# Three PSUM banks for the maximum tiles, batch steps in the value product's bank, and inverse roots of seven batches by a power on GpSimd

## The chip, the cores and the metric

The kernel runs on one core of one Trainium2 chip. The time is device microseconds of that core, the median of the runs.

## The reference

A pre-norm transformer layer on x of shape 8 x 512 x 128 in float32. `xn` is the layer norm of x. For each of 16 heads there are keys and queries of width 128 and values of width 8; scores q k / sqrt(128) under a causal mask, softmax, times v, the heads joined and multiplied by Wp, plus bp, plus x. The result is normed again: each row is centred and multiplied by 1/sqrt(variance + 1e-5). Then follows a mixture of experts: a shared feed-forward part, and 8 routed experts of which each row takes the 2 with the highest sigmoid of its logit, weighted by the normalised scores. Both are added to the row.

```
x = x + attention(layernorm(x))
x = x + shared(layernorm(x)) + sum over top-2 experts of w * down(silu(gate) * up)
```

## The kernel before, in words

The five engines run one program each, all laid out over the same numbered **slots** (`for t in range(SLOTS)`). There are 128 heads in all (8 batches x 16 heads, `UNITS`). In slot t:

- TensorE projects head t (L982 to L984, three float16 products: high times high, high times low, low times high) into bank 0. Then it scores head t - 10 for the softmax in three tiles (L1040 to L1042, banks 3 to 5), and between these tiles head t - 1 for its row maxima in three tiles k = 0, 1, 2 (L1019), with 512, 384 + 128 and 256 columns. Tile number n = 3u + k goes to bank 1 or 2, by n % 2, and waits until tile n - 2 has been reduced.
- ScalarE copies the projection to `qh` (L1264) and makes the exponentials of head t - 10 (L1299).
- VectorE writes the low half `ql` from the bank and `qh` (L1399), and reduces the maximum tiles (L1427, with an accumulator read that belongs to each). The next projection waits for `ql`.
- GpSimd zeroes what is above the diagonal of the exponentials (L914, L916).

Every fourth slot (t = 3 modulo 4, from slot 15: `PV_AT`) TensorE first multiplies four heads' exponentials with the values (`weigh_values`, L1056) into bank 6, and ScalarE copies the bank to `oT` (L1289) and stores it. In these slots VectorE reduces the maxima last, after all other work of the slot; in the others it reduces them ahead of that work. One slot earlier (t = 2 modulo 4, from slot 6) TensorE transposes the row maxima of four heads (L1215, "low"), VectorE casts them to `lowT` (L1407), and SyncE takes them through HBM into row 0 of `qh`.

The work that follows a batch is spread over the slots after its last head by hand-written offsets (`STEPS` for batches 0 to 6, `LAST_STEPS` for batch 7, `PART_STEPS` for the sorting of rows by expert), counted from slot 29 + 16b: "rinv" on VectorE (L1486), "mult" on GpSimd (L937), "proj" on TensorE (L1074) and VectorE (L1366), "stats" and "aggr" on VectorE (L1495, L1499), then the inverse root of the variance on VectorE: a seed from the bits (L108 to L111), three Newton steps (L116 to L119) in slots +6 and +7, a scaling (L1506). "norm" (+8) writes `hn` on GpSimd (L944), "split" (+10) its high half on ScalarE (L1252) and its low half on VectorE (L1391), and "logits" (+14) the router's product. "count", "rank" and "place" give each row its place among its expert's rows (L1104, L1114 to L1118, L1553 to L1572). All small products of this kind, "low", "proj", "logits", "count", "rank", the shared weights' transposes (L1007, slots 8 and 9) and the sum of the weights' squares, use bank 7 in turn: `turn` makes each wait until the last was taken (`t_taken`), and who reads it waits for `t_filled`.

```
T_USES = sorted([(LOW_AT + GROUP * g, "low", g) for g in range(GROUPS)] + [(W_SUM_AT, "w_sum", 0)]
X_BANK, V_BANK, SCALE_LINKS = (3, 4), (5, 6), 6
```

In slots 1 to 8 the batches are transposed (L992) and their values made (L1001, banks 5 and 6 by turns). GpSimd adds the bias to x in slots 11 to 18 (L908), and VectorE makes low halves of the projection's weights (L1432) until slot 13. From slot 138 (`FFN_AT`) on the feed-forward part runs, in banks 0 to 7, beside the last batch's steps.

## Time and profile before

| | |
|---|---|
| median of 3 runs | 730.77 us (729.43 to 732.49) |
| span of the profiled execution | 730.7 us, and no other time is given for that execution |
| TensorE busy (matmuls) | 654.0 us |
| VectorE busy | 541.8 us |
| ScalarE busy | 456.8 us |
| GpSimd busy | 310.2 us |
| first and last projection (L982) | 27.8 and 501.4 us |

In the profile PE is TensorE's matmuls, PEld its weight loads, DVE VectorE, ACT ScalarE, POOL GpSimd and SP SyncE. Lines are those of the kernel before. Matmuls overlap, so what one adds to the time is the distance between two starts, not its own duration.

### The profile page before, as it was taken

Reading aid. Unit: us, or ns where it says so; the run is one execution under the profiler, and the core shown is the slowest. Engines: PE = TensorE matmul, PEld = TensorE weight load, DVE = VectorE, ACT = ScalarE, POOL = GpSimd, SP = SyncE. Lnnn points to the kernel's source line nnn. Section 1 sums busy time; section 2 is a strip of 40 time slices with the busy share of each in tenths; the row PEclk is TensorE's granted clock in tenths of the full one; section 3 lists DMA queues with packets and bytes.
Section 4 is the critical chain, followed back from the end, with each engine's and each line's share of the span. In section 5 each row is a group of like instructions: output and inputs, shape, how many; then the busy total and the mean of one; then the engine's idle time right before and its main releaser. Section 6 shows DMA issues by size and latency. Waiting matters only on the chain.

```text
span 730.7 us, 16418 instructions
## 1 busy us (share of the span) xinstructions
PE 654.0 (90%) x5432; PEld 398.4 (55%) x5432; DVE 541.8 (74%) x1903; ACT 456.8 (63%) x816; POOL 310.2 (42%) x512
## 2 busy tenths in 40 slices
PE   7488999999999999998899999999986779899992
PEld 6264455545554554554445455455565568777652
DVE  6699877787788778788877877868546655567796
ACT  3376676767667776765676776666762545565651
POOL 4493531314123223221477522313465356565773
PEclk9699999999999999999999999999998889999997
DMA  9100443621122101221132111021444257695424
GB/s 255 53 2 20 133 128 105 175 77 45 49 74 44 32 32 42 77 70 37 49 93 85 45 51 42 17 44 64 102 107 107 73 117 145 126 164 120 110 60 126
DMA packets 102768, 60.24 MB, mean 82 GB/s; under 512 B 44568, under 2 KB 94640, under 8 KB 102688
## 3 DMA queue, kind: packets, MB, share of 16 engines
q1 hardware_dynamic: 66144, 28.22, 16.2%
q10 hardware_dynamic: 32336, 22.29, 10.4%
q0 software_dynamic: 4208, 8.69, 4.6%
q8 instruction: 47, 0.77, 0.4%
q14 instruction: 33, 0.27, 0.1%
HBM read 19.62 MB, written 30.77 MB: 69 GB/s over the span
## 4 chain that ended last, share of the span: by engine, by line
PE 63%; DVE 17%; ACT 6%; issue 6%; another core or an unknown queue 2%; POOL 1%; ACTq 0%; DVEq 0%; POOLq 0%
PE bank L1019 8%; PE bank L1040 7%; PE bank L1056 7%; PE bank L1042 6%; PE bank L1041 6%; DVE junk L1427 5%; PE bank L1136 4%; PE bank L1138 4%; PE bank L1137 4%; PE bank L982 3%; PE bank L984 3%; PE bank L983 3%; DVE ql L1399 3%; ACT p_sb L1299 2%
## 5 line engine op out<-in xcount | busy, mean ns | idle before, releaser
L1299 ACT ACTIVATE p_sb<-bank,inv_scale 128x512 f32<-128x512 f32 (+1 forms) x384 | 222.0, 614 | 40.6 <-PE bank L1042 33.3
L1427 DVE CUSTOM_DVE_ANT_0 junk<-bank,causal 128x512 bf16<-128x512 f32 (+3 forms) x512 | 221.8, 483 | 31.4 <-PE bank L1019 29.0
L914 POOL TENSOR_SCALAR_AFFINE_SELECT p_sb<-p_sb 128x384 f32<-128x384 f32 x128 | 67.0, 524 | 306.5 <-ACT p_sb L1299 305.9
L1041 PE MATMUL bank<-ql,ah 128*128 128x512 f16 (+3 forms) x512 | 153.4, 300 | 0.0
L1042 PE MATMUL bank<-qh,al 128*128 128x512 f16 (+3 forms) x512 | 153.0, 300 | 0.0
L1019 PE MATMUL bank<-ah,qh 128*128 128x512 f16 (+3 forms) x512 | 132.5, 303 | 21.8 <-DVE low L1427 20.3
L1040 PE MATMUL bank<-qh,ah 128*128 128x512 f16 (+3 forms) x512 | 147.2, 300 | 0.8 <-ACT p_sb L1299 0.8
L1399 DVE TENSOR_TENSOR ql<-bank,qh 128x512 f16<-128x512 f32 x128 | 88.5, 691 | 64.7 <-ACT qh L1264 61.3
L1264 ACT ACTIVATE qh<-bank 128x512 f16<-128x512 f32 x128 | 76.5, 597 | 62.4 <-PE bank L984 60.3
L1611 DVE SCALAR_TENSOR_TENSOR al<-bank,gu_scale,ah 128x512 f32<-128x512 f32 x69 | 51.6, 748 | 61.3 <-ACT ah L1330 41.9
L1019 PEld LDWEIGHTS bank<-ah,qh 128*128 128x128 f16 x512 | 50.1, 98 | 79.7 <-DVE low L1427 47.6
L1330 ACT ACTIVATE ah<-bank,inv_gate 128x512 f32<-128x512 f32 x69 | 47.4, 686 | 68.9 <-PE bank L1138 40.9
L962 POOL DMA_INDIRECT p_sb<-ys_dram,place x64 | 69.9, 1092 | 37.2 <-PE bank L1138 14.2
L953 POOL DMA_INDIRECT xs_dram<-rows,place x64 | 65.6, 1025 | 42.4 <-issue 14.4
L1056 PE MATMUL bank<-p_sb,v_sb 128*9 128x512 f32 (+3 forms) x1024 | 74.9, 433 | 0.3 <-POOL p_sb L916 0.3
L1040 PEld LDWEIGHTS bank<-qh,ah 128*128 128x128 f16 x512 | 50.2, 98 | 40.8 <-issue 8.3
L1042 PEld LDWEIGHTS bank<-qh,al 128*128 128x128 f16 x512 | 50.1, 98 | 25.0 <-issue 0.3
L1136 PE MATMUL bank<-mh,wh 128*128 128x256 f16 x212 | 60.3, 284 | 3.3 <-issue 1.6
L1138 PE MATMUL bank<-mh,wl 128*128 128x256 f16 x212 | 60.2, 284 | 2.1 <-issue 2.0
L1041 PEld LDWEIGHTS bank<-ql,ah 128*128 128x128 f16 x512 | 50.2, 98 | 21.7 <-issue 0.3
L1137 PE MATMUL bank<-ml,wh 128*128 128x256 f16 x212 | 60.0, 283 | 1.7 <-issue 1.7
L1174 PE MATMUL bank<-wh,qh 128*128 (+1 forms) x276 | 53.6, 227 | 6.3 <-ACT ql L1325 2.7
(247 smaller groups left out, 1130.2 us busy)
## 6 DMA issues: line engine op xcount, KB each, us to landing
o_dram<-oT ACTq DMA_DIRECT2D x32, 256.0 KB, 2.3
ys_dram<-ql ACTq DMA_DIRECT2D x25, 256.0 KB
xs_dram<-causal ACTq DMA_DIRECT2D x6, 832.0 KB, 4.8
wst<-in_Wkqv SPq DMA_DIRECT2D x8, 264.0 KB, 5.0
x_sb<-in_x SPq DMA_DIRECT2D x8, 256.0 KB, 5.8
out<-x_sb SPq DMA_DIRECT2D x8, 256.0 KB
o_all<-o_dram SPq DMA_DIRECT2D x7, 256.0 KB
r_all<-r_dram SPq DMA_DIRECT2D x7, 256.0 KB
```

The lines of the kernel that those rows point to most:

```text
L1019: last = nc.tensor.matmul(m.psum[M_BANK[n % 2]][:, at:at + w], qh[:, u % RING, i * P:(i + 1) * P], m.ah[:, seg(b, N, w)], start=True, stop ...
L1040: nc.tensor.matmul(bank, m.ah[:, keys], qh[:, s, c * P:N], start=True, stop=False)
L1041: nc.tensor.matmul(bank, m.ah[:, keys], ql[:, s, c * P:N], start=False, stop=False)
L1042: last = nc.tensor.matmul(bank, m.al[:, keys], qh[:, s, c * P:N], start=False, stop=True)
L1056: last = nc.tensor.matmul(m.psum[O_BANK][32 * j:32 * j + V1, c * P:N], m.v_sb[:, v // H * TB + c, v % H, :], p_sb[v % P_RING][:, P_AT[c]:P ...
L1136: nc.tensor.matmul(out, hi, x_h, start=True, stop=False)
L1137: nc.tensor.matmul(out, hi, x_l, start=False, stop=False)
L1138: return nc.tensor.matmul(out, lo, x_h, start=False, stop=True)
L1264: nc.scalar.activation(qh[:, t % RING, :], m.psum[Q_BANK][:, :], ACT.Copy).then_inc(qh_ready, 1)
L1299: nc.scalar.activation(p_sb[v % P_RING][:, S_AT[k]:S_AT[k] + S_WIDTH[k]], m.psum[S_BANK[k]][:, 0:S_WIDTH[k]], ACT.Exp, scale=m.inv_scale[: ...
L1399: nc.vector.tensor_tensor(ql[:, t % RING, :], m.psum[Q_BANK][:, :], qh[:, t % RING, :], ALU.subtract).then_inc(ql_ready, 1)
L1427: last = nc.vector.tensor_tensor_reduce(out=junk[:, (3 * u + k) % 2, at:at + w], in0=m.psum[M_BANK[(3 * u + k) % 2]][:, at:at + w], in1=m. ...
```

## The change

The maximum tiles get one bank each, 1, 2 and 7, and tile k waits for tile k of the head before. Until slot 138 the small products that used bank 7 use bank 6, the value product's; from then on bank 7. So `turn` now also waits, until slot 138, for the last copy of the value product (in slots up to 9 for the values' copy or the bank's clearing), after it for the last maximum; and `weigh_values`, and the values' products that use bank 6, wait until the small products before them are taken. The steps that met the value product's slots move: logits +14 to +15, rank and place +26 to +27, send +27 to +28, the shared weights' transposes from slots 8 and 9 to 11 and 12. `same_head` now shares its memory with `ones`, and is made by GpSimd in slot 50 instead of slot 10, by two instructions instead of three. `junk` is [128, 1280], a part for each tile. For batches 0 to 6 the inverse root leaves VectorE; GpSimd computes (variance + eps) ** -0.5 ahead of "norm" in two instructions on 128 x 4. Batch 7 keeps the old way.

```diff
+        self.same_head = self.ones
...
-STEPS = {"rinv": 0, "mult": 2, "proj": 4, "stats": 6, "aggr": 6, "newton0": 6, "newton1": 7, "newton2": 7, "norm": 8, "split": 10, "logits": 14}
+STEPS = {"rinv": 0, "mult": 2, "proj": 4, "stats": 6, "aggr": 6, "newton0": 6, "newton1": 7, "newton2": 7, "norm": 8, "split": 10, "logits": 15}
...
-PART_STEPS = {"sort": 18, "weigh": 22, "count": 23, "rank": 26, "place": 26, "expert": 30, "send": 27}
+PART_STEPS = {"sort": 18, "weigh": 22, "count": 23, "rank": 27, "place": 27, "expert": 30, "send": 28}
...
+SAME_HEAD_AT = W_SUM_AT + 2
...
-SHARED_T_AT = B
+SHARED_T_AT = LAG + 1
...
-    Q_BANK, M_BANK, S_BANK, O_BANK, T_BANK = 0, (1, 2), (3, 4, 5), 6, 7
+    Q_BANK, M_BANK, S_BANK, O_BANK, T_BANK = 0, (1, 2, 7), (3, 4, 5), 6, 7
...
+    def t_bank(t):
+
+        return m.psum[O_BANK if t < FFN_AT else T_BANK]
...
+            nc.gpsimd.memset(minus_half[:, :], -0.5).then_inc(low_clear, 1)
+            pool.wait_ge(low_clear, 3)
...
                 if (b := batch_at("norm", t)) is not None and b < B - 1:
+                    pool.wait_ge(spread_known, b + 1)
+                    nc.gpsimd.tensor_scalar(raised[:, :], m.stats[:, seg(b, TB), 1], EPS, None, ALU.add).then_inc(var_raised, 1)
+                    pool.wait_ge(var_raised, b + 1)
+                    nc.gpsimd.tensor_tensor(m.rstd[:, seg(b, TB)], raised[:, :], minus_half[:, :], ALU.pow).then_inc(rstd_ready, 1)
                     pool.wait_ge(rstd_ready, b + 1)
...
+                if V_BANK[b % 2] == O_BANK and turns_before(b + 2) > 0:
+                    pe.wait_ge(t_taken, turns_before(b + 2))
...
-                if n >= 2:
-                    pe.wait_ge(max_ready, n - 1)
+                if u >= 1:
+                    pe.wait_ge(max_ready, n - 2)
...
             def weigh_values(g):
                 pe.wait_ge(p_masked, 2 * GROUP * (g + 1))
 
+                pe.wait_ge(t_taken, turns_before(min(PV_AT + GROUP * g, FFN_AT)))
...
             def turn(name, n):
+                at = T_USES[T_TURN[name, n]][0]
                 if T_TURN[name, n] > 0:
                     pe.wait_ge(t_taken, T_TURN[name, n])
+                if at >= FFN_AT:
+                    pe.wait_ge(max_ready, 3 * UNITS)
+                elif at > PV_AT:
+                    pe.wait_ge(oT_ready, weighed_before(at))
+                elif at > B + 1:
+                    pe.wait_ge(o_clear, 1)
+                else:
+                    pe.wait_ge(v_ready, at - at % 2 - 2)
...
-                    post.link(last)
-                    rsqrt_seed(nc, post.link, m.stats[:, seg(b, TB), 1], var[:, :], m.rstd[:, seg(b, TB)], tmp[:, :])
+                    if b < B - 1:
+                        last.then_inc(spread_known, 1)
+                    else:
+                        post.link(last)
+                        rsqrt_seed(nc, post.link, m.stats[:, seg(b, TB), 1], var[:, :], m.rstd[:, seg(b, TB)], tmp[:, :])
                 for step in range(RSQRT_STEPS):
-                    if (b := batch_at(f"newton{step}", t)) is not None:
+                    if (b := batch_at(f"newton{step}", t)) == B - 1:
```

## Rows read from the trace of the kernel before

**Rows 1.** the busy shares of the whole span (engine, us, share, instructions).

```profile
PE 654.0 (90%) x5432; PEld 398.4 (55%) x5432; DVE 541.8 (74%) x1903; ACT 456.8 (63%) x816; POOL 310.2 (42%) x512
```

**Rows 2.** busy us by stretch, 79.2 to 501.4; then PE clock, DMA share, GB/s.

```profile
79.20:501.40 422.20, 408.09 (x3179) 215.25 (x3180) 330.65 (x1281) 291.06 (x515) 141.39 (x282) 1.00 0.23 66
```

**Rows 3.** the waits from 79.2 to 501.4: us, times, longest.

```profile
DVE ql L1399 <- ACT qh L1264: 55.8, 95, 1.4
...
PEld bank L1019 <- DVE low L1427: 36.6, 85, 2.8
...
PE bank L1019 <- DVE low L1427: 13.1, 19, 2.5
```

**Rows 4.** timeline of slot 40 and its neighbours: start, length, [idle before].

```profile
172.50 0.38 PE L982 MATMUL bank<-ah,mh 128*128 128x512 f16 x1
...
175.10 0.27 PE L1042 MATMUL bank<-qh,al 128*128 128x256 f16 x1
...
175.19 0.08 DVE L1427 DVE_READ_ACCUMULATOR2_ANT low<- 128x1 f32 x1
...
175.32 0.10 PEld L1019 LDWEIGHTS bank<-ah,qh 128*128 128x128 f16 x1 [0.23 <-DVE low L1427]
...
175.33 0.28 PE L1019 MATMUL bank<-ah,qh 128*128 128x256 f16 x1
...
175.45 0.38 PE L982 MATMUL bank<-ah,mh 128*128 128x512 f16 x1
...
176.22 0.08 DVE L1427 DVE_READ_ACCUMULATOR2_ANT low<- 128x1 f32 x1
...
176.92 0.69 DVE L1399 TENSOR_TENSOR ql<-bank,qh 128x512 f16<-128x512 f32 x1 [0.62 <-ACT qh L1264]
...
178.28 0.28 PE L1019 MATMUL bank<-ah,qh 128*128 128x256 f16 x1
```

**Rows 5.** timeline of slot 35, the first with a batch's statistics.

```profile
155.68 0.17 DVE L108 TENSOR_SCALAR var<-stats 128x4 f32<-128x4 f32 x1
...
156.96 0.69 DVE L1427 CUSTOM_DVE_ANT_0 junk<-bank,causal 128x512 bf16<-128x512 f32 x1
...
157.72 0.28 PE L1019 MATMUL bank<-ah,qh 128*128 128x256 f16 x1 [0.90 <-DVE low L1427]
```

**Rows 6.** TensorE at the end of slot 83, and the stretch behind it.

```profile
339.82 0.39 PE L1019 MATMUL bank<-ah,qh 128*128 128x256 f16 x1 [2.51 <-DVE low L1427]
...
340.00:344.00 4.00, 4.00 (x18) 1.85 (x17) 2.38 (x10) 1.35 (x3) 0.00 (x0) 0.62 0.00 0
```

**Rows 7.** VectorE's chain of rank and place, first and last instruction.

```profile
527.32 0.20 DVE L1553 TENSOR_TENSOR above<-ranks,full_tiles 128x48 f32<-128x48 f32 x1
...
529.86 0.18 DVE L1572 CAST place<-slot 128x24 int32<-128x24 f32 x1
```

**Rows 8.** timeline of hn, its split and oT, batches 0 and 6.

```profile
165.03 3.16 POOL L944 TENSOR_SCALAR hn<-x_sb,stats,rstd 128x128 f32<-128x128 f32 x4
...
168.64 0.62 ACT L1252 ACTIVATE rows<-hn 128x512 f16<-128x512 f32 x1
...
170.45 0.60 ACT L1289 ACTIVATE oT<-bank 128x512 f32<-128x512 f32 x1 [1.19 <-PE bank L1056]
...
526.05 0.63 ACT L1252 ACTIVATE rows<-hn 128x512 f16<-128x512 f32 x1 [2.31 <-POOL hn L944]
```

**Rows 9.** timeline of slot 6, the values' product and the cast.

```profile
50.59 1.06 PE L1001 MATMUL bank<-wv,wh 128*128 128x128 f32 x8
...
51.48 0.27 DVE L1407 CAST lowT<-bank 16x128 f16<-16x128 f32 x1
```

**Rows 10.** the waits of the whole span.

```profile
DVE ql L1399 <- ACT qh L1264: 61.3, 106, 1.5
```

**Rows 11.** groups of GpSimd by shape: busy us, mean ns.

```profile
L310 POOL COPY wv<-wst 128x16 f32<-128x16 f32 x8 | 1.8, 223 | 5.6 <-DMA wst<-in_Wkqv 5.6
...
L908 POOL TENSOR_TENSOR x_sb<-x_sb,bp_bc 128x512 f32<-128x512 f32 x8 | 10.2, 1273 | 0.0
```

More of the change, by code:

```diff
@@ L533, with turns_before, weighed_before @@
 T_TURN = {(name, n): i for i, (_, name, n) in enumerate(T_USES)}
+def turns_before(t):
+    return sum(1 for at, _, _ in T_USES if at < t)
+def weighed_before(t):
+    return sum(1 for g in range(GROUPS) if PV_AT + GROUP * g < t)
+assert not any(group_at(at, PV_AT) is not None for at, _, _ in T_USES if at < FFN_AT)
 X_RING, GU_RING, LATE, DEEP = 4, 6, 4, 3
@@ L725, in body @@
     var = sb("var2", [P, TB], F32)
+    raised = sb("raised", [P, TB], F32)
+    minus_half = sb("minus_half", [P, TB], F32)
     tmp = sb("tmp2", [P, TB], F32)
@@ L1013, in score_for_max @@
                     pe.wait_ge(qh_ready, u + 1)
-                if n >= 2:
-                    pe.wait_ge(max_ready, n - 1)
+                if u >= 1:
+                    pe.wait_ge(max_ready, n - 2)
                 for i, at in MAX_TILES[k]:
                     w = (i + 1) * P
-                    last = nc.tensor.matmul(m.psum[M_BANK[n % 2]][:, at:at + w], qh[:, u % RING, i * P:(i + 1) * P], m.ah[:, seg(b, N, w)], start=True, stop=True)
+                    last = nc.tensor.matmul(m.psum[M_BANK[k]][:, at:at + w], qh[:, u % RING, i * P:(i + 1) * P], m.ah[:, seg(b, N, w)], start=True, stop=True)
                 last.then_inc(max_scored, 1)
@@ L1067, in after_attention @@
                     pe.wait_ge(w_sq_ready, 1)
-                    nc.tensor.matmul(bank_t[:, 0:KINDS], m.ones[:, :], w_sq[:, :], start=True, stop=True).then_inc(t_filled, 1)
+                    nc.tensor.matmul(t_bank(t)[:, 0:KINDS], m.ones[:, :], w_sq[:, :], start=True, stop=True).then_inc(t_filled, 1)
                 if (b := batch_at("proj", t)) is not None:
@@ L1073, in after_attention @@
                     for i in range(TB):
-                        last = nc.tensor.matmul(bank_t[:, i * P:(i + 1) * P], onT[:, i * P:(i + 1) * P], m.wp[:, :], start=True, stop=True)
+                        last = nc.tensor.matmul(t_bank(t)[:, i * P:(i + 1) * P], onT[:, i * P:(i + 1) * P], m.wp[:, :], start=True, stop=True)
                     last.then_inc(t_filled, 1)
@@ L1078, in after_attention @@
                     pe.wait_ge(late_r_ready, 1)
-                    pe.wait_ge(same_head_made, 3)
-                    nc.tensor.matmul(bank_t[:, :], m.same_head[:, :], r_all[:, :], start=True, stop=True).then_inc(t_filled, 1)
+                    pe.wait_ge(same_head_made, 2)
+                    nc.tensor.matmul(t_bank(t)[:, :], m.same_head[:, :], r_all[:, :], start=True, stop=True).then_inc(t_filled, 1)
                 if late_at("late", t):
@@ L1084, in after_attention @@
                     for i in range(TB):
-                        last = nc.tensor.transpose(bank_t[:, i * P:(i + 1) * P], hn[:, i, :], m.ident[:, :])
+                        last = nc.tensor.transpose(t_bank(t)[:, i * P:(i + 1) * P], hn[:, i, :], m.ident[:, :])
                     last.then_inc(t_filled, 1)
@@ L1103, in after_attention @@
                     for c, (t0, t1) in enumerate(CHUNKS[g]):
-                        last = nc.tensor.matmul(bank_t[0:(t1 - t0) * E, c * P:(c + 1) * P], picked[:, t0:t1, :].rearrange("p t e -> p (t e)"), m.ones16[:, :], start=True, stop=True)
+                        last = nc.tensor.matmul(t_bank(t)[0:(t1 - t0) * E, c * P:(c + 1) * P], picked[:, t0:t1, :].rearrange("p t e -> p (t e)"), m.ones16[:, :], start=True, stop=True)
                     last.then_inc(t_filled, 1)
@@ L1110, in after_attention @@
                     for c, (t0, t1) in enumerate(CHUNKS[g]):
-                        rank = bank_t[:, c * P:c * P + rows[c]]
+                        rank = t_bank(t)[:, c * P:c * P + rows[c]]
                         for d in range(c):
@@ L1117, in after_attention @@
                     for c in range(len(rows)):
-                        last = nc.tensor.matmul(bank_t[:, at:at + E], totals[0:rows[c], base + c, :], m.earlier[0:rows[c], CHUNK, :], start=(c == 0), stop=(c == len(rows) - 1))
+                        last = nc.tensor.matmul(t_bank(t)[:, at:at + E], totals[0:rows[c], base + c, :], m.earlier[0:rows[c], CHUNK, :], start=(c == 0), stop=(c == len(rows) - 1))
                     last.then_inc(t_filled, 1)
@@ L1214, in _ @@
                     turn("low", g)
-                    nc.tensor.transpose(bank_t[:, 0:P], low[g % 2][:, :], m.ident[:, :]).then_inc(t_filled, 1)
+                    nc.tensor.transpose(t_bank(t)[:, 0:P], low[g % 2][:, :], m.ident[:, :]).then_inc(t_filled, 1)
                 if 1 <= t < B:
```

44 lines of the change are left out of this document (20 added, 24 removed).

## The prediction

> **What bounds the kernel now.** Read the busy shares first: TensorE is busy 90% of the span, VectorE 74%, ScalarE 63%, GpSimd 42% [rows 1]. Then the stretches: from 79.2 to 501.4 us, heads 15 to 126, TensorE is busy 408.1 of 422.2 us at a granted clock of 1.00 (2.4 GHz) [rows 2]. So TensorE sets the pace there, and what can be won is its stalls. The waits of that stretch name one: the matmuls of L1019 (scores for the row maxima) wait for VectorE's reductions of L1427, 36.6 us in 85 waits seen at the weight load and 13.1 us in 19 seen at the matmul [rows 3].
>
> These two are not to be added, since one stall shows at both. And the 85 waits start too early: a weight load is issued ahead. In an ordinary slot the last score matmul starts at 175.10 and would have let L1019 start at 175.21 (each 256-column matmul follows the last by 0.11); VectorE reads its accumulator from 175.19 to 175.27, L1019 starts at 175.33, and the next slot at 175.45 [rows 4]. The loss is 0.12 us of a slot of 2.95 (172.50 to 175.45), where the weight load's wait says 0.23. With 0.11 taken off each, 36.6 - 85 x 0.11 = 27.3 us is the real loss in this stretch.
>
> **The three maximum banks.** Two banks serve three tiles per head, so tile 2 waits for tile 0 of its own head. In rows 4 that tile is read just when it is wanted. With a bank per tile it waits for tile 2 of the head before, which VectorE has left at 176.30 (176.22 + 0.08) where the next slot's L1019 starts at 178.28. The margin goes from -0.12 to about 1.8 us.
> - Ordinary slots: about 84 outside the value product's own, 84 x 0.12 = 10.1 us. I take all. Next in line is ql: VectorE is done with a slot at 176.30 and starts ql at 176.92 [rows 4], when qh comes; 0.62 us less the 0.12 that the slot shrinks leaves 0.5, so VectorE still keeps up.
> - Slots with batch work on VectorE hold the other 27.3 - 10.1 = 17.2 us. In slot 35 the maxima start at 156.96 and L1019 waits 0.90 [rows 5]. The third bank alone covers this. The worst is slot 83, with a wait of 2.51 us, after which the clock is granted at 0.62 (part of the time at 1.2 GHz) for 4 us [rows 6]; those 4 us hold some 1.5 us more, if matmuls run 0.62 as fast, in a slot that the 27.3 us don't count.
>
> What stays: rank and place move to the plain slot 88, behind the maxima. Their chain takes 2.7 us (527.32 to 530.04) [rows 7]; the free time behind the maxima is 0.5, and ql may end some 0.8 us later before the next projection waits. 2.7 - 1.3 = 1.4 us stays, about what it costs now. For other heavy slots where VectorE's own work is too long I leave 2.1 us. Gain of the stretch: 27.3 - 1.4 - 2.1 = **23.8 us**, and I leave the 1.5 us of the clock as a reserve.
>
> Bounds of this term: 10.1 (only the even stall goes) and 28.8 (all, with the clock).
>
> **The shared bank.** The low transpose sits one slot ahead of the value product, and the other steps move to other slots, so each pair lies a slot apart. VectorE takes such a tile some 1.5 us before the product wants the bank; ScalarE copies oT right when the product ends, two slots ahead of the next low transpose. The logits, count and rank steps come one slot behind the product, whose copy starts at 170.45 [rows 8], in the same slot. Price 0; if a take is late, each of 28 groups loses up to the 0.27 us of a cast [rows 9], 7.6 us.
>
> **The first 15 slots.** There VectorE is nearly full, and its wait for qh is 61.3 - 55.8 = 5.5 us outside the stretch [rows 3, 10], since a late L1019 delays the next projection. I take half, 2.7 us won. Against it: in slot 6 the values' matmuls start at 50.59 but must now wait until lowT is cast at 51.75 [rows 9], 1.2 us; and the shared weights' transposes move into slots 11 and 12, for which I take 0.5 us between nothing and another 1.2 of the same kind. Net **+1.0**, between -1.2 and +3.
>
> **The inverse root.** From VectorE seven times: seed, Newton steps and scaling, thirteen instructions; the part in slot 35 is 155.68 to 156.96, 1.28 us [rows 5]. That sits in the stalls counted above, so it gets no credit of its own: either part alone removes them, and they overlap. To GpSimd come an add and a power, each 128x4. No row shows a power. Nearest in size is the copy of 128x16, 0.22 us; nearest as a two-input operation is L908 over 512 elements, 1.27 us [rows 11]. Two instructions: 0.45 to 2.5 us. I take 1.0, since four elements are nearer the copy, but a power is more than a copy. Nothing excludes that it is far dearer, which is a rival below.
>
> What hides it: GpSimd writes hn from 165.03 to 168.19, ScalarE takes it at 168.64 and then idles 1.19 us before oT [rows 8]. Slack 0.45 + 1.19 = 1.64, less 0.12 for a shorter slot: 1.5 us. Under it, batches 0 to 5 cost nothing. Behind the waits on GpSimd are the next head's masks, which the product wants several slots later. Batch 6 has no slack: ScalarE waits 2.31 us for hn at 526.05 [rows 8] on the chain that ended last. There the 1.0 us is paid: **-1.0**.
>
> The Trainium skill (GPSIMD Engine Reference, Specifications and Performance versus the Vector engine) says that GpSimd is about half as fast at elementwise work and shares its SBUF interfaces with VectorE where an instruction has two SBUF inputs. By it the move is the wrong way; at four elements it would still be covered by the slack.
>
> **The sum.** 23.8 + 1.0 - 1.0 = 23.8 us off the profiled execution's 730.7, **706.9 us**. The median of the runs is 730.77, so nothing shifts. Work after 501.4 is unchanged and simply starts earlier.
>
> **The rivals.**
> 1. *The power is dear.* Place: GpSimd ahead of hn; hn late, so ScalarE's split, oT and the exponentials late. Price for an add and power of X: 6 x (X - 1.5) + (X - 1.0) more than my sum. At X = 3, 718; at 6, 739. It cancels the gain at 7X = 33.8, X = 4.8 us, and from 5.4 the kernel is slower by over 0.5%. For: no row prices a power, and a GpSimd pass can cost 1.27. Against: it is four elements. Chance 0.13 for X over 2.5, of which 0.07 beyond 5.4 and 0.02 within 0.5% of no change.
> 2. *A new wait eats half.* The shared bank loses 0.27 us per group (7.6), and 3 to 4 us of heavy slots stay because ql, not the maxima, is what is late there: 718. For: VectorE's margin is but 0.5. Against: the places lie a slot apart. Chance 0.13.
> 3. *TensorE is not what is short.* The stalls turn up elsewhere, at qh or the exponentials, because the same VectorE and ScalarE latencies close the loop: 728, within 0.5%. Against: TensorE is busy 408.1 of 422.2 us, and VectorE 330.7 of them [rows 2]. Chance 0.04.
>
> 4. *The first power alone is slow.* If it takes as long as the four instructions of hn, 3.16 us [rows 8], slot 37 is late by 3.16 - 1.5 = 1.7 us once: 708.6. Against: nothing in the trace shows a first instruction of its kind to be longer. Chance 0.05. The Trainium skill (GPSIMD Engine Reference, Instruction dispatch) has the first call of newly loaded code pay about 6 us; by it slot 37 would lose some 4.5 us, an estimate from that page, for 711.4.
>
> The forecast holds 0.65. Half a per cent, 3.7 us, is what can be told from no change. Faster: 0.65 + 0.13 + 0.05 + 0.04 of rival 1 = 0.87; same 0.04 + 0.02 = 0.06; slower 0.07. The range runs from 701 (all stalls, with the clock) to 722 (rival 2, and the power up to 3.5 us).
>
> **What would show it.** Right: L1019's waits for L1427 nearly gone from the stretch, ordinary slots 2.82 to 2.83 us, no idle time before L1019 in slot 83 and no clock below 1.00 behind it, the stretch from head 15's projection to the last near 398 us. Power: the duration of its row, and whether ScalarE waits for hn more than once. Shared bank: no waits of L1056 or L1215 on oT or lowT. Wrong: ordinary slots still 2.95, or as much idle time in front of L982.

## The result, and the profile after

The kernel after takes 708.49 us (707.27 to 710.94 in 4 runs) where the kernel before takes 730.96 (729.43 to 732.49 in 4 runs): a ratio of 0.9683, 95% interval 0.9647 to 0.9719. The forecast was 706.9 us, and the range 701 to 722 holds the result. The profiled execution has a span of 709.0 us and a time of its own of 710.94, so it is 2.5 us above the median; spans below are compared with spans (730.7 before).

Where the 21.7 us between the spans come from, counted at the first matmul of each head's projection (the interval from one head's projection to the next is called a slot here; a value slot is one with the value product, a low slot the one ahead of it, with the transpose of the maxima, and any other is an ordinary slot):

| Stretch | Before | After | Difference |
|---|---|---|---|
| start to head 0's projection | 27.8 | 28.8 | +1.0 |
| slots 0 to 14 | 51.5 | 49.4 | -2.1 |
| slots 15 to 126 | 422.2 | 395.4 | -26.8 |
| last projection to the end | 229.3 | 235.5 | +6.2 |

So the stretch with heads gained 3 us more than forecast, and the part behind it lost some 5 us more. The busy shares of the kernel after, which answer to [rows 1], from its profile page:

```profile
PE 642.9 (91%) x5432; PEld 406.0 (57%) x5432; DVE 525.1 (74%) x1812; ACT 454.1 (64%) x816; POOL 318.1 (45%) x526
```

VectorE has 91 instructions fewer, GpSimd 14 more. The stretches by busy time (us, then busy us and count of TensorE, its weight loads, VectorE, ScalarE, GpSimd, then clock, DMA share, GB/s), the first of which answers to [rows 2]:

```profile
78.13:473.48 395.35, 393.66 (x3181) 220.65 (x3179) 317.91 (x1205) 287.94 (x516) 150.16 (x296) 1.00 0.24 71
473.48:709.00 235.52, 190.76 (x1888) 142.32 (x1885) 145.13 (x351) 123.05 (x214) 126.35 (x137) 0.94 0.46 108
```

TensorE now idles 1.7 us of the 395.4; before it was 14.1 of 422.2. What it waited for there, from the waits of this stretch at the matmuls (us, times, longest), against the 13.1 us in 19 of [rows 3]:

```profile
PE bank L1006 <- DVE ql L1435: 1.3, 1, 1.3
...
PE bank L1045 <- DVE low L1463: 0.2, 1, 0.2
```

L1045 is the old L1019, L1463 the old L1427, L1006 the old L982. The 36.6 us in 85 waits at L1019's weight load are gone from this stretch. The one wait that is left, 1.3 us, is in slot 89, where VectorE's chain of rank and place stands ahead of ql. The same ordinary slot 40 as in [rows 4], from the timeline:

```profile
166.84 0.38 PE L1006 MATMUL bank<-ah,mh 128*128 128x512 f16 x1
...
169.44 0.27 PE L1068 MATMUL bank<-qh,al 128*128 128x256 f16 x1
...
169.55 0.27 PE L1045 MATMUL bank<-ah,qh 128*128 128x256 f16 x1
169.55 0.10 PEld L1006 LDWEIGHTS bank<-ah,mh 128*128 128x128 f16 x1
169.66 0.38 PE L1006 MATMUL bank<-ah,mh 128*128 128x512 f16 x1
```

L1045's last tile now follows the last score matmul by 0.11 us (169.44, 169.55) and the slot is 2.82 us long where it was 2.95. Slot 83 has gone from 7.95 to 5.20, the length of a plain slot with a value product.

The inverse root, from the groups by shape (busy us, mean ns):

```profile
L962 POOL TENSOR_TENSOR rstd<-raised,minus_half 128x4 f32<-128x4 f32 x7 | 7.3, 1045 | 0.6
L960 POOL TENSOR_SCALAR raised<-stats 128x4 f32<-128x4 f32 x7 | 1.7, 238 | 0.0
```

and for batch 0 from the timeline of GpSimd (this view ends after two of hn's four instructions):

```profile
160.12 0.24 POOL L960 TENSOR_SCALAR raised<-stats 128x4 f32<-128x4 f32 x1
160.45 1.05 POOL L962 TENSOR_TENSOR rstd<-raised,minus_half 128x4 f32<-128x4 f32 x1
161.61 1.61 POOL L968 TENSOR_SCALAR hn<-x_sb,stats,rstd 128x128 f32<-128x128 f32 x2
```

A power on 128x4 costs 1.05 us, and with the add and the two handovers hn starts 1.49 us later (160.12 to 161.61) than it would without them. The first power is as long as the others.

### The profile page after: what moved, and what is told of

It is laid out like the page before. It is cut to its first block, busy times and chain, and to the rows that moved or that the text cites. A ratio compares the mean times of both kernels' runs of the same rounds, so it can differ in the third digit from the quotient of the medians.

```text
span 709.0 us, 16346 instructions
## 1 busy us (share of the span) xinstructions
PE 642.9 (91%) x5432; PEld 406.0 (57%) x5432; DVE 525.1 (74%) x1812; ACT 454.1 (64%) x816; POOL 318.1 (45%) x526
## 4 chain that ended last, share of the span: by engine, by line
PE 69%; DVE 9%; POOL 7%; issue 5%; ACT 4%; another core or an unknown queue 2%; ACTq 0%; DVEq 0%; POOLq 0%
PE bank L1066 8%; PE bank L1083 8%; PE bank L1045 8%; PE bank L1068 8%; PE bank L1067 8%; PE bank L1174 4%; PE bank L1172 4%; PE bank L1006 3%; PE bank L1007 3%; PE bank L1008 3%; PE bank L1173 3%; POOL xs_dram L977 3%; DVE junk L1463 2%; PE bank L1210 2%; PE bank L1211 2%
## 5 line engine op out<-in xcount | busy, mean ns | idle before, releaser
L1463 DVE CUSTOM_DVE_ANT_0 junk<-bank,causal 128x512 bf16<-128x512 f32 (+3 forms) x512 | 221.8, 483 | 27.1 <-PE bank L1045 26.3
L1045 PE MATMUL bank<-ah,qh 128*128 128x512 f16 (+3 forms) x512 | 130.1, 301 | 0.4 <-DVE low L1463 0.4
L986 POOL DMA_INDIRECT p_sb<-ys_dram,place x64 | 68.3, 1066 | 38.4 <-PE bank L1174 15.3
L1083 PE MATMUL bank<-p_sb,v_sb 128*9 128x512 f32 (+3 forms) x1024 | 74.9, 433 | 0.3 <-POOL p_sb L937 0.3
L1045 PEld LDWEIGHTS bank<-ah,qh 128*128 128x128 f16 x512 | 50.2, 98 | 34.3 <-issue 1.6
L1210 PE MATMUL bank<-wh,qh 128*128 (+1 forms) x276 | 53.3, 226 | 13.5 <-ACT ql L1361 7.5
```

Of the source, the lines that this page charges most:

```text
L1045: last = nc.tensor.matmul(m.psum[M_BANK[k]][:, at:at + w], qh[:, u % RING, i * P:(i + 1) * P], m.ah[:, seg(b, N, w)], start=True, stop=True)
L1083: last = nc.tensor.matmul(m.psum[O_BANK][32 * j:32 * j + V1, c * P:N], m.v_sb[:, v // H * TB + c, v % H, :], p_sb[v % P_RING][:, P_AT[c]:P ...
L1463: last = nc.vector.tensor_tensor_reduce(out=junk[:, S_AT[k] + at:S_AT[k] + at + w], in0=m.psum[M_BANK[k]][:, at:at + w], in1=m.causal[:, N ...
```

## The experiments

Twelve runs were made of ten different kernels, in three sets of four, each set on one chip beside the kernel before. Six powers and six powers with the values swapped were measured in two of the sets, and the kernel after once more. Ratios are to the kernel before of the same set, whose median was 732.19 us for the first set and 734.88 for the other two. The chips differ (the kernel before takes 732.19 us on one and 734.88 on the others), so between sets the ratios are to be compared and not the times. "To last" is the time from head 15's projection to the last one, "tail" from the last projection to the end of the span, both of the profiled run.

| Kernel | us | Ratio (95%) | To last | Tail |
|---|---|---|---|---|
| before | 732.19 / 734.88 | 1 | 422.2 | 229.3 |
| after, first measurement | 708.49 | 0.9683 (0.9647-0.9719) | 395.4 | 235.5 |
| banks only | 707.26 | 0.9667 (0.9632-0.9702) | 399.1 | 227.6 |
| power only | 730.05 | 0.9972 (0.9948-0.9996) | 416.2 | 234.3 |
| two banks | 726.49 | 0.9940 (0.9912-0.9969) | 413.3 | 229.1 |
| six powers | 703.97 | 0.9625 (0.9592-0.9658) | 395.2 | 228.1 |
| six powers, values swapped | 706.05 | 0.9603 (0.9574-0.9632) | 396.4 | 229.6 |
| powers thrice | 717.80 | 0.9776 (0.9740-0.9811) | 405.8 | 230.4 |
| last batch by a power too | 707.76 | 0.9617 (0.9573-0.9660) | 395.4 | 231.7 |
| place later | 711.09 | 0.9666 (0.9623-0.9708) | 395.0 | 237.7 |
| batch 6's power alone | 714.50 | 0.9732 (0.9705-0.9759) | 399.0 | 236.4 |
| after, again | 709.59 | 0.9651 (0.9631-0.9671) | 396.1 | 235.1 |
| six powers, again | 706.28 | 0.9611 (0.9591-0.9631) | 396.1 | 230.1 |
| values swapped, again | 704.30 | 0.9583 (0.9564-0.9602) | 397.4 | 231.6 |

### One part at a time: the banks only

```diff
                 if (b := batch_at("norm", t)) is not None and b < B - 1:
-                    pool.wait_ge(spread_known, b + 1)
-                    nc.gpsimd.tensor_scalar(raised[:, :], m.stats[:, seg(b, TB), 1], EPS, None, ALU.add).then_inc(var_raised, 1)
-                    pool.wait_ge(var_raised, b + 1)
-                    nc.gpsimd.tensor_tensor(m.rstd[:, seg(b, TB)], raised[:, :], minus_half[:, :], ALU.pow).then_inc(rstd_ready, 1)
...
-                    if (b := batch_at(f"newton{step}", t)) == B - 1:
+                    if (b := batch_at(f"newton{step}", t)) is not None:
```

(the seed and the closing scale come back for all batches in the same way).

> The three banks and the batch steps in the value product's bank, but all eight inverse roots on VectorE as before. Theory (the banks carry the gain, either part alone frees the heavy slots): every slot is as short as with the whole change, 2.82 ordinary and 5.20 value slots, slot 83 included; the chain of Newton steps hides behind TensorE; batch 6's 1.5 us in the tail comes back, so 705.5 to 708.5, most likely 707. Rival (the root's move is what freed the heavy slots): slots 35, 51, 67, 83 and 99 keep 0.7 to 2.7 us each of their stalls, some 12 to 17 us in all, so 718 to 725.

Measured: 707.26 us, 0.9667. The time is the theory's, the slots are so only nearly: slots 35, 51, 67, 83, 87 and 99 are all 5.20, but slots 84 (4.50 instead of 2.88), 85 (3.72 for 2.82) and 53 (3.49 for 2.83) stay long, and the stretch is 399.1 us, 3.8 above the kernel after. The timeline of TensorE in slot 84:

```profile
326.87 0.38 PE L1041 MATMUL bank<-ah,qh 128*128 128x512 f16 x1 [1.02 <-DVE low L1459]
```

and of VectorE ahead of it (a Newton step, and the chain of the weights behind it):

```profile
324.03 0.15 DVE L119 SCALAR_TENSOR_TENSOR rstd<-tmp,rstd 128x4 f32<-128x4 f32 x1
...
325.74 0.25 DVE L1580 TENSOR_TENSOR weight<-top 128x12 f32<-128x12 f32 x2
326.02 0.69 DVE L1459 CUSTOM_DVE_ANT_0 junk<-bank,causal 128x512 bf16<-128x512 f32 x1
```

The third bank gives TensorE one slot of room, not more: VectorE is more than a slot late here, the Newton steps being part of what is queued ahead of the maxima. So taking seven roots off VectorE is worth these 3.8 us when the banks are there, and 2.9 in the one pair below that was measured on one chip.

### The power only

```diff
@@ the kernel before
-                    post.link(last)
-                    rsqrt_seed(nc, post.link, m.stats[:, seg(b, TB), 1], var[:, :], m.rstd[:, seg(b, TB)], tmp[:, :])
+                    if b < B - 1:
+                        last.then_inc(spread_known, 1)
+                    else:
+                        post.link(last)
+                        rsqrt_seed(nc, post.link, m.stats[:, seg(b, TB), 1], var[:, :], m.rstd[:, seg(b, TB)], tmp[:, :])
```

with the add and the power on GpSimd as in the change.

> The kernel before with seven of its inverse roots by a power on Pool and nothing else of the change. Theory (either part alone frees the heavy slots): slots 35, 51, 67, 83, 87 and 99 fall to 5.20 to 5.4 us, the ordinary slots stay at 2.95 with their wait of TensorE for the reduction; 17 us less in the stretch, 1.5 more for batch 6 behind it, so 713 to 718, most likely 715. Rival (the heavy slots stall on the second bank's turn whatever VectorE has in its queue there): they keep most of it and the time is 724 to 731.

Measured: 730.05 us, 0.9972: the rival was right in the time, and the theory wrong. The slots show neither reason alone. 35, 51, 67 and 99 do fall to 5.20 (from 5.93 to 6.56) and 84 and 85 to 3.14 and 2.95. But 83 keeps 6.33, 87 grows from 6.83 to 8.29 and 88 from 2.95 to 4.50, and 39, 71 and 103 each grow by 0.5 to 0.6. In slot 88 TensorE is busy throughout, at a granted clock of 0.62: that growth is the clock behind the wait of slot 87. Slot 84's old length had held the same kind of fall, with 0.65 granted. From TensorE's timeline:

```profile
334.73 0.28 PE L1027 MATMUL bank<-ah,qh 128*128 128x256 f16 x1 [0.95 <-DVE low L1435]
352.25 0.28 PE L1027 MATMUL bank<-ah,qh 128*128 128x256 f16 x1 [2.82 <-DVE low L1435]
```

Slot 83 still has statistics, weight splits and the sort of a whole part ahead of its maxima; slot 87 has rank and place, and now in front of them VectorE's own wait for the split of hn, 1.06 us, since hn comes later:

```profile
347.51 0.69 DVE L1399 SCALAR_TENSOR_TENSOR rows<-hn,rows 128x512 f16<-128x512 f32 x1 [1.06 <-ACT rows L1260]
```

So with two banks the power takes away one queue and lengthens another: it gains 6.0 us in the stretch, and 5.0 of them are lost again in the tail (229.3 to 234.3).

### The third bank taken away

```diff
-    Q_BANK, M_BANK, S_BANK, O_BANK, T_BANK = 0, (1, 2, 7), (3, 4, 5), 6, 7
+    Q_BANK, M_BANK, S_BANK, O_BANK, T_BANK = 0, (1, 2), (3, 4, 5), 6, 7
...
-                if u >= 1:
-                    pe.wait_ge(max_ready, n - 2)
+                if n >= 2:
+                    pe.wait_ge(max_ready, n - 1)
...
-                    last = nc.tensor.matmul(m.psum[M_BANK[k]][:, at:at + w], qh[:, u % RING, i * P:(i + 1) * P], m.ah[:, seg(b, N, w)], start=True, stop=True)
+                    last = nc.tensor.matmul(m.psum[M_BANK[n % 2]][:, at:at + w], qh[:, u % RING, i * P:(i + 1) * P], m.ah[:, seg(b, N, w)], start=True, stop=True)
```

> The whole change but for the third bank: the maximum tiles alternate between two banks as before, the batch steps stay in the value product's bank and the power on Pool. Theory: 10 us of ordinary slots come back (0.12 to 0.13 each in some 84), and what the third bank alone gives in the heavy slots; 717 to 722, most likely 719, with TensorE's wait for VectorE before the maximum products back at some 30 us or more. Rival (the third bank gives the ordinary slots nothing, their shortening comes from elsewhere, such as the batch steps): within 2 us of the kernel after, 707 to 711.

Measured: 726.49 us, 0.9940, above the expected 717 to 722. The direction is the theory's: ordinary slots are back at 2.95, low slots at 3.14. The size is larger, since the third bank is worth 17.9 us in the stretch (413.3 against 395.4) and 3.8 in the first 15 slots (53.2 against 49.4), of which only some 10 are the even stall, the 0.12 us or so that every ordinary slot loses. TensorE's waits for VectorE before the maxima came back as 12.9 us at the matmul and 38.0 at the weight load (over the whole span, where the kernel after has 0.4 and 0.8):

```profile
PEld bank L1045 <- DVE low L1463: 38.0, 90, 1.9
PE bank L1045 <- DVE low L1463: 12.9, 20, 1.6
```

Beside the power-only kernel this one also prices the shared bank and the moved steps: they cost 1.7 us in the first 15 slots (slots 6 and 10 are 1.4 longer each) and gain 2.9 in the stretch, mostly because rank and place left the value slot (87 to 89 together are 13.5 us for 15.7) and the logits steps left theirs (43, 59 and so on are 5.20 for 5.48).

### Batch 6's root back on VectorE

```diff
                 if (b := batch_at("norm", t)) is not None and b < B - 1:
+                    if b < B - 2:
+                        pool.wait_ge(spread_known, b + 1)
...
-                    if (b := batch_at(f"newton{step}", t)) == B - 1:
+                    if (b := batch_at(f"newton{step}", t)) is not None and b >= B - 2:
```

> The kernel after with batch 6's inverse root back on VectorE, six powers left. Theory (that power stands on the path behind the last projection and, as TensorE idles there, costs clock too): the last exponentials come 1.5 to 3 us earlier after the last projection (33.8 in the kernel after, 30.7 before) and the time is 705.5 to 707.5, most likely 706.5. Rival (the offset is set by the later gaps in the feed forward part, not by batch 6): the start of the feed forward part moves, the end does not, and the time is 708 to 709.5.

Measured: 703.97 us, 0.9625, which is 1.5 us below the range given, and beside the kernel after on one chip (third set) 706.28 us against 709.59. The direction is the theory's, and the last exponentials do come 3.1 us earlier. In the kernel after, the chain in the tail reads, for ScalarE and TensorE:

```profile
499.59 0.63 ACT L1288 ACTIVATE rows<-hn 128x512 f16<-128x512 f32 x1 [3.79 <-POOL hn L968]
...
500.85 0.20 PE L1150 MATMUL bank<-earlier,totals 96*128 96x96 f16 x1 [1.76 <-ACT oT L1325]
```

and with batch 6's root on VectorE:

```profile
496.08 0.63 ACT L1289 ACTIVATE rows<-hn 128x512 f16<-128x512 f32 x1 [2.30 <-POOL hn L969]
...
497.34 0.20 PE L1151 MATMUL bank<-earlier,totals 96*128 96x96 f16 x1 [0.27 <-ACT oT L1326]
```

ScalarE waits 1.49 us longer for hn, which is the handover of the power; oT and the exponentials queue behind it, so TensorE stands 1.49 us longer too. Then the clock: the windows from 25 us after the last projection, two of 5 us each, first of the kernel after:

```profile
498.50:503.50 5.00, 2.92 (x21) 1.72 (x20) 2.81 (x10) 3.79 (x7) 2.58 (x6) 0.92 0.46 132
503.50:508.50 5.00, 4.67 (x29) 2.69 (x31) 0.51 (x3) 3.58 (x6) 1.75 (x5) 0.74 0.23 52
```

with six powers:

```profile
496.50:501.50 5.00, 4.41 (x35) 2.67 (x34) 3.31 (x12) 4.95 (x10) 1.81 (x6) 1.00 0.47 132
501.50:506.50 5.00, 4.66 (x54) 2.68 (x53) 0.75 (x1) 2.61 (x4) 3.50 (x5) 1.00 0.32 81
```

and with two banks and the same power for batch 6:

```profile
519.30:524.30 5.00, 2.92 (x23) 1.67 (x21) 2.74 (x10) 3.80 (x7) 2.65 (x6) 1.00 0.47 133
524.30:529.30 5.00, 4.66 (x48) 2.58 (x49) 1.33 (x4) 4.20 (x7) 3.00 (x6) 1.00 0.26 61
```

TensorE is busy 2.92 us of the first window in the first and the third, 4.41 in the second. In the kernel after the granted clock then falls to 0.92 and 0.74, which is 3.4 us in all at 1.2 GHz (0.8 in the first window, 2.6 in the second), and TensorE gets 29 matmuls done in the second window where it does 48 in the two-bank kernel, which idles as long and keeps its clock, and 54 with six powers. ScalarE's first silu of the feed-forward part dates the effect in every profile: 30.7 us after the last projection in the nine profiles of kernels with batch 6's root on VectorE, 32.2 in the two-bank kernel (the handover alone), and 33.8 or 33.9 in the four with the power and a clock below 1.00 (after twice, power only, batch 6's power alone). Their tails are 234.3 to 236.4 us. The two-bank kernel's is 229.1, within those without the power (227.6 to 231.7, place later aside). So of the 3.1 us by which the first silu is late, 1.5 are the handover and 1.6 the clock. (3.4 us at half the clock hold what full speed does in 1.7, so 1.7 is the most that it can cost.) From the silu to the end these four take 200.6 to 202.5 us and the others, place later aside, 196.9 to 201.0. This further difference of some 2 us, which makes up the 5 us of tail seen in the profiles, isn't explained. And that the fall of the clock is worth 1.6 us rests on a single profile of the two-bank kernel.

### The six powers' worth, and batch 6's alone

The edit is shown against the kernel with six powers.

```diff
-                    if b < B - 2:
+                    if b == B - 2:
...
-                    if (b := batch_at(f"newton{step}", t)) is not None and b >= B - 2:
+                    if (b := batch_at(f"newton{step}", t)) is not None and b != B - 2:
```

> Three banks, and a power on POOL for batch 6 alone; the batches 0 to 5 have their roots on VectorE as before. Theory (batch 6's power is all loss, the other six are all gain): the slots are those of the kernel with the banks only (84, 85, 53, 37, 69 and 101 longer by 3.8 us together than in the kernel after), the tail is that of the kernel after (first silu of the feed forward part 33.8 us after the last projection, not 30.7), so it is the slowest of this set, 3 to 4 us above the kernel after on the same chip, near 712. Rival (batch 6's power costs its 1.5 us and the rest of the loss in the tail is chance of the runs): 1.5 us above the kernel with the banks only, near the kernel after, 708 to 709.

> The kernel after, unchanged, on the same chip as the three others of this set. Theory: 4 to 5 us above the kernel with six powers, 3 to 4 below the one with batch 6's power alone. Rival (batch 6's power costs only its handover): 1.5 us above the kernel with six powers.

> The kernel with six powers, batch 6's root on VectorE, beside the kernel after on one chip. Theory: 0.6 per cent (4 to 5 us) faster than it. Rival: 0.2 per cent.

Measured on one chip: 714.50, 709.59 and 706.28 us. The order is the theory's; the sizes are not quite. Batch 6's power costs 3.3 us (709.59 to 706.28, ratios 0.9651 and 0.9611, whose intervals just meet, while the slowest of the five runs with six powers, 706.98, is below the fastest of the other five, 707.85). That lies between the theory's 4 to 5 and the rival's 1.5, and agrees with the 3.1 us seen at the first silu. Between sets the ratios give 4.2 us (0.9683 less 0.9625) and 4.8 (0.9732 less 0.9667) for the same power. The other six powers gain 4.9 us (714.50 to 709.59, intervals apart), of which 2.9 to 3.6 can be read in the stretch (399.0 against 396.1 and 395.4). The two nearly cancel in the kernel after, which is why it does not differ from the banks only: 0.9651 and 0.9683 against 0.9667.

### How much room the power has

The edit is against the kernel with six powers.

```diff
-                        nc.gpsimd.tensor_tensor(m.rstd[:, seg(b, TB)], raised[:, :], minus_half[:, :], ALU.pow).then_inc(rstd_ready, 1)
+                        nc.gpsimd.tensor_tensor(m.rstd[:, seg(b, TB)], raised[:, :], minus_half[:, :], ALU.pow).then_inc(var_raised, 1)
+                        pool.wait_ge(var_raised, 3 * b + 2)
+                        nc.gpsimd.tensor_tensor(m.rstd[:, seg(b, TB)], raised[:, :], minus_half[:, :], ALU.pow).then_inc(var_raised, 1)
+                        pool.wait_ge(var_raised, 3 * b + 3)
+                        nc.gpsimd.tensor_tensor(m.rstd[:, seg(b, TB)], raised[:, :], minus_half[:, :], ALU.pow).then_inc(rstd_ready, 1)
```

> The kernel with six powers, each of them run three times in a row, so 2.09 us more on POOL ahead of each batch's rows. By the prediction's price (six times what the power exceeds its slack of 1.5 us; the handover now takes 1.48) that costs 6 times 2.07, 12.4 us, so 716. Rival (a batch's rows have more room than 1.5 us since three banks leave VectorE and ScalarE ahead of TensorE): under 2 us, 704 to 706, with ScalarE's wait for the rows some 2 us longer each time and no value slot above 5.3.

Measured: 717.80 us, 0.9776. Against 0.9625 and 0.9611 for the same kernel with single powers that is 1.5% of 734.88 us, 11 to 12 us, where the prediction's formula gives 12.4. Slots 40, 56, 72, 88, 104 and 120 are longer by 1.8, 1.3, 1.7, 1.6, 2.2 and 1.3 us, 10.0 in all, each at a granted clock of 1.00. The timeline at slot 40:

```profile
167.20 0.63 ACT L1293 ACTIVATE rows<-hn 128x512 f16<-128x512 f32 x1 [3.90 <-POOL hn L973]
...
169.04 0.38 PE L1071 MATMUL bank<-qh,ah 128*128 128x512 f16 x1 [1.17 <-ACT p_sb L1340]
```

ScalarE stands 3.90 us for hn with oT and the exponentials behind it, and TensorE waits for the exponentials. From the first power's start to hn it is 3.33 us in that slot (160.67 to 164.00) where a single power takes 1.16 (160.45 to 161.61 above), so 2.17 us are added, and 10.0/6 = 1.67 of them is lost: 1.49 + 2.17 - 1.67 = 2.0 us is the room for add and power, on the mean of the six. The prediction had 1.5. The single power uses three quarters of it.

### Slot 6: the values in the other bank

Slot 6 went from 3.39 us to 6.50 in the kernel after. Its rows, which answer to [rows 9]:

```profile
51.43 0.27 DVE L1443 CAST lowT<-bank 16x128 f16<-16x128 f32 x1
...
51.84 1.81 PE L1027 MATMUL bank<-wv,wh 128*128 128x128 f32 x8 [1.48 <-DVE lowT L1443]
...
53.45 1.27 PE L1045 MATMUL bank<-ah,qh 128*128 128x512 f16 x4
```

The wait is 1.48 us, and behind it the same matmuls take longer: 1.81 us for eight of the values' product (1.06 before) and 1.27 for the four of the maxima (0.71 in the kernel with six powers and the swap, below). The granted clock of slot 6 is 0.81:

```profile
48.01:54.51 6.50, 4.21 (x22) 2.89 (x21) 4.36 (x14) 3.12 (x7) 6.42 (x7) 0.81 0.02 5
```

The first profile of six powers has the same wait of 1.48 us and a clock of 1.00 in slots 6 and 7, which take 5.34 and 2.53 us there against 6.50 and 3.02: the fall of the clock costs 1.7 us. It does not always come in slot 6. Of the nine profiles with the shared bank and the values not swapped, five show it there, three in slot 10 (4.5 to 4.6 us there, for 2.94) and one in neither.

The swap, against the kernel with six powers:

```diff
-    X_BANK, V_BANK, SCALE_LINKS = (3, 4), (5, 6), 6
+    X_BANK, V_BANK, SCALE_LINKS = (3, 4), (6, 5), 6
...
-                    pe.wait_ge(v_ready, at - at % 2 - 2)
+                    pe.wait_ge(v_ready, at - at % 2 - 1)
```

> The kernel with six powers, and the values of the batches 0, 2, 4, 6 instead of 1, 3, 5, 7 in the bank that the transposes of the minima share, so that in slot 6 the transpose and batch 5's values lie in different banks. Theory (slot 6 grew from 3.39 to 5.34 and 6.50 us because TensorE waits 1.48 us for VectorE's copy out of the shared bank and its clock falls behind the wait): slot 6 falls to 3.0 to 3.6 us, the time by 1.5 to 2.5 us to 702, unless the wait reappears in slot 7, where batch 6's values follow the transpose into the same bank; there the copy is a slot old. Rival (the first slots are bound by the chain of transposes, ScalarE's copies and POOL's rows, whatever the bank): slots 5 to 8 keep their sum and the time stays within 0.7 us of 704.

> Six powers and the banks of the values swapped, beside the same on one chip. Theory: slots 5 to 8 together are 1.5 to 2 us shorter than in the kernel with six powers, and the time is 1 to 2 us below it, the fastest of this set, since nothing behind the first slots changes. Rival: the feed forward part takes up the gain, no difference.

Measured: 706.05 us, 0.9603, where the kernel without the swap had 0.9625 in the first set, and on the third set 704.30 us, 0.9583, against 706.28, 0.9611. The timeline of slot 6 in the second of them:

```profile
50.27 1.06 PE L1028 MATMUL bank<-wv,wh 128*128 128x128 f32 x8
...
51.16 0.71 PE L1046 MATMUL bank<-ah,qh 128*128 128x512 f16 x4
51.50 0.27 DVE L1444 CAST lowT<-bank 16x128 f16<-16x128 f32 x1
51.70 0.38 PE L1007 MATMUL bank<-ah,mh 128*128 128x512 f16 x1
```

The product no longer waits for the cast, the clock stays, and the slot takes 3.62 us. Slot 7 gets longer (3.69 for 2.53 to 3.02), so slots 5 to 8 together are only 0.6 us shorter than with six powers (13.46 for 14.02), and not the 1.5 to 2 expected. Slots 0 to 14 take 47.1 to 47.2 us with the swap and 48.2 to 49.7 without; most of that is the clock, which falls in slot 6 or 10 in all but one of the profiles without the swap, and in neither slot in the three with it. This has the lowest ratio of the study, 0.9583 (0.9564 to 0.9602), though its interval overlaps with that of six powers. Its lead of 2.0 us over the one without the swap is about what such runs can tell; both pairs of runs point the same way.

### The last batch by a power too

The edit is against the kernel with six powers.

```diff
+                if late_at("norm", t):
+                    pool.wait_ge(spread_known, B - 1)
+                    nc.gpsimd.tensor_scalar(raised[:, :], m.stats[:, seg(B - 1, TB), 1], EPS, None, ALU.add).then_inc(var_raised, 1)
+                    pool.wait_ge(var_raised, B - 1)
+                    nc.gpsimd.tensor_tensor(m.rstd[:, seg(B - 1, TB)], raised[:, :], minus_half[:, :], ALU.pow).then_inc(rstd_ready, 1)
                 for g, i, k in sends_at(t):
```

> The kernel with six powers, and the last batch's root also by a power on POOL (batch 6's alone stays on VectorE). TensorE waits 4.2 us for that batch's normalised rows, behind a chain of 14 small instructions on VectorE. Theory (what counts is the length of the chain against the handover): the chain takes 3.9 us from 527.85 to 531.73 with two feed forward instructions between, add and power 1.5, so the rows come up to 1.5 us earlier and the time falls by up to 1.5 to 702.5 to 704. Rival (POOL issues row sends at that point, 1.0 to 1.4 us each behind TensorE's progress, and the power queues behind one of them): the rows come 0 to 3 us later and the time is 704 to 708.

Measured: 707.76 us, 0.9617, the same as with six powers. TensorE's wait for that batch's rows fell from 4.2 to 2.0 us, so the handover is shorter than the chain, as the theory has it. But GpSimd reaches the add early and stands in front of it, with its row sends behind:

```profile
530.01 0.24 POOL L974 TENSOR_SCALAR raised<-stats 128x4 f32<-128x4 f32 x1 [5.24 <-DVE stats L1542]
530.33 1.04 POOL L976 TENSOR_TENSOR rstd<-raised,minus_half 128x4 f32<-128x4 f32 x1
531.57 1.17 POOL L984 DMA_INDIRECT xs_dram<-rows,place  x1 [0.20 <-issue]
```

The queueing is the other way round from the rival: not the power behind a send, the sends behind the power's wait, 5.24 us and another 1.5. Nothing is left of the gain at the end. Whether the held sends are what took it wasn't tested.

### Place three slots later

The edit is against the kernel with six powers and the values swapped.

```diff
-PART_STEPS = {"sort": 18, "weigh": 22, "count": 23, "rank": 27, "place": 27, "expert": 30, "send": 28}
+PART_STEPS = {"sort": 18, "weigh": 22, "count": 23, "rank": 27, "place": 30, "expert": 30, "send": 31}
```

> The kernel with six powers and the swapped values, and the place step of the first two parts three slots later, in a value slot, with the sends behind it. Theory (slot 89 is 1.2 to 1.5 us too long because VectorE has the place step's eight small instructions ahead of the next low half, and a value slot has over 2 us of room on VectorE): slot 89 falls to 2.9 to 3.2 us and the time by 1.0 to 1.5 us more than with the swap alone, to 700.5. Rival (the sends that follow later collide with the batch rows or with the feed forward part): no gain or 1 to 3 us of loss in the later stages.

Measured: 711.09 us, 0.9666, against 706.05 us, 0.9603, for the same kernel without it: 5.0 us slower. Slot 89 did fall, from 4.15 to 3.32, and the later stages took it back many times over, more than the rival's 1 to 3 us: the tail is 237.7 us for 229.6. GpSimd's sends wait 21.2 us for TensorE's progress there where they waited 9.6, and the sends end later (the last starts at 588.7 for 585.1, though the last projection is 2.5 us earlier). From the groups' waits of the send, this kernel:

```profile
  PE bank L1175: 21.2, 8
```

and without the move:

```profile
  PE bank L1175: 9.6, 5
```

In the program the sends of the feed-forward part wait for a unit of TensorE's work, so sends pushed out of the head slots are paced by it and add waits to the queue. Whether that is all of the loss wasn't tested.

## Why the prediction was right, point by point

- **The total**, 706.9: measured 709.0 in the span and 708.49 by the median. That it is so near is partly luck: the stretch gained 3.0 us more than its term, and what lies behind it lost 5.2 us more than its own.
- **What bounds.** TensorE's stalls, right: in the stretch its idle time went from 14.1 to 1.7 us.
- **Ordinary slots**, 84 x 0.12 = 10.1: right. The ordinary slot went from 2.95 to 2.82 and the low slot from 3.14 to 2.93; eight ordinary slots don't change and five of those with the logits step are 0.17 longer, so the 74 slots that had no stall of batch work gave 9.6 us together. And ql still keeps up, as the margin of 0.5 us said: VectorE still waits 0.49 us for qh ahead of it, and TensorE waits for ql once in the stretch, 1.3 us in slot 89.
- **The sum of the stretch**, 23.8: measured 26.8, length 395.4 for the "near 398". The 27.3 us of stall were read rightly with the 0.11 us taken off each wait. The terms that were off are the 2.1 us left for heavy slots, of which nothing stayed, and the 1.5 us of clock behind slot 83, left as a reserve, which came: slot 84, with a clock of 0.65 before, is 4.38 to 2.88 us. 27.3 + 1.5 - 1.5 (slot 89) is 27.3, against 26.8.
- **Rank and place**, 1.4 us stay: slot 89 is 4.31 us, 1.49 above an ordinary one.
- **"Either part alone removes them"**, of the heavy slots' stalls: wrong, and the step that failed. The power alone took 6.0 us of the stretch, the banks alone 23.1, both 26.8. The prediction read the stall of slot 35, where the root's 1.28 us is indeed all of it, and let it stand for slots 83 and 87, where sort, statistics or rank and place hold VectorE as well. The sum did not hang on this, since both parts were in.
- **The power's price**, X = 1.0 within 0.45 to 2.5: measured 1.49 from the add's start to hn (0.24, 1.05 and two handovers of a tenth). In batches 0 and 6 the add starts when GpSimd is done with its masks, not when the statistics are ready. Under the slack, as said: in batches 0 to 5 no value slot is longer for it, though ScalarE waits 10.8 us for hn in all six together.
- **The slack**, 1.5 us: measured 2.0. The first rival's formula, 6 times what exceeds the slack, gave 12.4 us for the tripled power where 11 to 12 were measured.
- **Batch 6**, -1.0: the term that was mis-sized, in kind. The handover of 1.5 us is there, but the loss at the end is 3.3 us by the medians and some 5 in the profile. Of these 3.1 are there at the first silu, 1.5 of handover and 1.6 of clock, which fell behind TensorE's longer stand; the rest of the profile's 5 stays open. The prediction priced the late instruction and not what TensorE's idle time does to the matmuls behind it, though [rows 6] had just shown that behind slot 83. "Work after 501.4 is unchanged and simply starts earlier" was wrong for the same reason.
- **The shared bank**, 0: right for the slots with value products. L1083 (the old L1056) never waits for the bank in the kernel after. It isn't free in the tail, where the rank's matmul in that bank waits for oT; yet the power-only kernel, with a bank of its own, loses as much there, its scores waiting 2.26 us for the exponentials. So the late ScalarE is enough without the shared bank.
- **The first 15 slots**, +1.0: measured 2.1 in the slots, less a start that is 1.0 later. The start varies from 27.7 to 30.0 us over the profiles, 27.7 to 27.9 in the three with two banks and 28.1 or more with three; the cause wasn't looked for. Slot 6 cost 3.1, not the 1.2 of the sum: 2.0 where the clock holds, as in the first profile of six powers, and 1.2 more with its fall. The other slots gave 5.2 (slot 1 alone 1.35, 12 to 14 together 2.0).
- **The fourth rival**, a slow first power: did not happen. The first took 1.05 us like the rest. The Trainium skill (GPSIMD Engine Reference, Instruction dispatch) has the first call of newly loaded code pay about 6 us; no row of these traces shows that for the power.
- **The second rival** at half size would have been a fair description of the tail: a new wait does eat something, but behind ScalarE and not at the bank.

What stays open: both kernels have, 33 to 36 and 47 to 49 us behind the last projection, two gaps in the chain that ended last, of 4.7 and 5.3 us before and 3.9 and 4.6 after, that end on no event the trace names. Tails vary by some 4 us between kernels that differ in nothing there (227.6 to 231.6); whether these gaps do it wasn't tried. And why the clock holds in the two-bank kernel after the same idle time can't be read from a trace.

## What to carry to other kernels

A buffer added where a consumer is read just when it is wanted is worth its even stall on every turn and all the uneven ones up to one turn's room; work taken off the consumer was worth little here while the buffer was missing, and added to its gain where the lateness exceeded that room. A step that is moved to an idle engine is free only under the slack of whoever takes its result, so price it batch by batch: six of these seven were a gain, and the seventh, where no work was left to hide it, cost two thirds of what the six brought (3.3 of 4.9 us). Where the delayed wait leaves TensorE standing, add the matmuls behind it at the lower clock to the price of the wait.

## What the runs showed of the hardware that was not expected

- 1.5 us more of idle time on TensorE was followed by a time at 1.2 GHz in four profiles of five: 0.81 to 0.92 granted in a stretch of 5 us and 0.74 to 0.85 in the next, and 1.00 in both in the fifth, at nearly the same busy time of the first (2.7 to 2.9 us of 5). In the nine profiles with 4.2 to 4.4 us busy there both are at 1.00. What decides between the four and the fifth isn't known.
- The same wait of 1.48 us in slot 6 was followed by a lower clock in some profiles of a kernel and not in others (six powers: 1.00 in slot 6 in both profiles, a fall in slot 10 in the second alone), so the position of such a fall can't be read off one profile.
- Every such fall that can be priced cost about the same: 1.4 us in slot 84 before (4.38 for an ordinary slot's 2.95), 1.6 in slot 88 of the power-only kernel (4.50 for 2.95), 1.7 in slots 6 and 7 after and in slot 10 of the second profile of six powers (4.59 for 2.94), and 1.6 ahead of the first silu.
- A power of two inputs over 128x4 on GpSimd takes some 1.0 us, an add with a constant of the same size 0.24: at this size the price goes by the operation.
